# Reload of the residual tile moved into the second batch's turn of the next group

## The reference

```
x = x + L0(x)      # per batch, one of 16 matrices 32x32 mixes the 32 rows
x = x + L1(x)      # x @ base_weight.T + bias + a low-rank adapter per batch
x = x + L2(x)      # paged attention, below
x = x + L3(x)      # as L0, with other weights

# L2: 32 query heads, 8 key/value heads, D = 128, fp32
q, k, v = x @ Wq.T, x @ Wk.T, x @ Wv.T          # q and k: RMS norm, then rotary embedding
kc, vc  = k_cache[block_table], v_cache[block_table]   # 16 pages of 32 positions per batch
scores  = q @ concat(kc, k).T * SCALE           # cached positions >= cache_seqlens are masked
o       = softmax(scores) @ concat(vc, v)
return    o @ Wo.T
```

## Time and profile before

| | us |
|---|---|
| median of 3 runs | 2405.72 |
| lowest and highest | 2402.29, 2407.57 |
| profiled execution | 2406.59 |
| its span | 2404.8 |
| PE busy | 2278.3 (95%) |
| DVE busy | 1766.7 (73%) |
| ACT busy | 1592.9 (66%) |
| mean granted TensorE clock | 0.975 |

### The profile page before, as it was taken

The page is one execution under the profiler, slowest core; times in us unless marked ns, Lnnn a source line. Parts: engine busy times, 40 slices in busy tenths (PEclk is TensorE's granted clock), DMA queues, the critical chain, the costliest instruction groups (busy, mean ns, idle before and its releaser), DMA issues.

```text
span 2404.8 us, 56518 instructions
## 1 busy us (share of the span) xinstructions
PE 2278.3 (95%) x15392; PEld 2026.5 (84%) x15392; DVE 1766.7 (73%) x5613; ACT 1592.9 (66%) x4413; POOL 543.0 (23%) x712
## 2 busy tenths in 40 slices
PE   8999999999998999989989989989989989999999
PEld 5688888888887898988988988988988989887777
DVE  3425777777778987977978978978878878876232
ACT  4324666666668887877877877877877878776221
POOL 1003444444442122111121221212212212110000
PEclk9999999999999999999999999999999999999999
DMA  4335333333348777676777777767767677774332
GB/s 164 94 109 163 101 98 101 119 99 98 101 123 282 251 253 233 225 253 221 233 244 237 225 230 249 232 218 247 234 221 257 216 230 246 224 237 173 112 131 100
DMA packets 347991, 456.02 MB, mean 190 GB/s; under 512 B 34538, under 2 KB 280874, under 8 KB 343726
## 3 DMA queue, kind: packets, MB, share of 16 engines
q1 hardware_dynamic: 308430, 315.83, 41.9%
q0 software_dynamic: 36864, 134.23, 16.4%
q10 hardware_dynamic: 2528, 4.29, 0.5%
HBM read 374.53 MB, written 79.69 MB: 189 GB/s over the span
## 4 chain that ended last, share of the span: by engine, by line
PE 61%; SPq 14%; DMA 9%; issue 8%; DVE 4%; ACT 3%; POOLq 0%; ACTq 0%; POOL 0%; DVEq 0%
PE oP L1209 11%; PE S L1209 10%; PE oP L1285 9%; SPq L379 8%; PE S L1303 7%; PE S L1252 7%; PE bank L1133 5%; DMA x_d<-regC 4%; SPq L377 4%; PE bank L1316 4%; DMA regK<-kT_cache 3%; PE oP L1133 3%; PE oP L1163 2%; DVE k_lo L998 2%; PE oP L1295 1%
## 5 line engine op out<-in xcount | busy, mean ns | idle before, releaser
L1285 PEld LDWEIGHTS oP<-regC,regK 128*128 128x128 f32 x4096 | 540.1, 195 | 37.4 <-issue 4.4
L1285 PE MATMUL oP<-regC,regK 128*128 128x128 f32 x4096 | 552.9, 279 | 1.1
L726 ACT CAST k_hi<-regK 128x544 fp32r<-128x544 f32 x512 | 331.3, 647 | 213.6 <-DMA regK<-kT_cache 109.3
L998 DVE TENSOR_TENSOR k_lo<-regK,k_hi 128x544 fp32r<-128x544 f32 x512 | 368.1, 719 | 98.5 <-ACT k_hi L726 98.3
L1013 DVE CUSTOM_DVE_ANT_0 regC<-S,mask 128x544 f32<-128x544 f32 x512 | 368.5, 720 | 73.1 <-issue 69.5
L1133 PE MATMUL bank<-ident,regC 128*128 128x128 f32 x2048 | 315.2, 277 | 84.9 <-ACT regC L786 84.9
L740 ACT ACTIVATE regC<-regC,nmx 128x544 f32<-128x544 f32 x512 | 387.7, 757 | 4.5 <-DVE nmx L1013 4.0
L1133 PEld LDWEIGHTS bank<-ident,regC 128*128 128x128 f32 x2048 | 247.9, 143 | 87.7 <-issue 87.7
L567 POOL TENSOR_TENSOR regC<-regC 128x256 f32<-128x256 f32 x320 | 245.2, 786 | 278.9 <-DVE regC L973 278.9
L786 ACT COPY regC<-bank 128x512 f32<-128x512 f32 x512 | 298.7, 583 | 5.0 <-PE bank L1133 5.0
L549 POOL DMA_INDIRECT regK<-v_cache,idx x256 | 266.6, 1042 | 91.8 <-issue 91.4
(11 more groups left out here) (136 smaller groups left out, 4319.7 us busy)
## 6 DMA issues: line engine op xcount, KB each, us to landing
regK<-kT_cache SPq DMA_DIRECT2D x1024, 128.0 KB
qkT_d<-regC SPq DMA_DIRECT2D x160, 256.0 KB, 2.3
regC<-qkT_d SPq DMA_DIRECT2D x64, 512.0 KB, 7.1
oT_d<-regC SPq DMA_DIRECT2D x64, 256.0 KB, 6.0
regK<-oT_d SPq DMA_DIRECT2D x16, 1024.0 KB, 5.2
regC<-wqk SPq DMA_DIRECT2D x10, 1024.0 KB, 5.2
v_d<-regC SPq DMA_DIRECT2D x32, 256.0 KB, 2.3
regK<-qkT_d SPq DMA_DIRECT2D x64, 128.0 KB
```

Source lines behind the costliest of these rows:

```text
L726: nc.scalar.copy(k_hi[u % 2].rearrange("p (s t) -> p s t", t=PSIZE), k_sb[b][:, :, h, :]).then_inc(s_khi, 1)
L998: nc.vector.tensor_tensor(lo, k_sb[b][:, :, h, :], hi.bitcast(F32), ALU.subtract).then_inc(s_klo, 1)
L1285: last = nc.tensor.matmul(oP[:, at:at + P], v_sb[b][:, m, h * D:(h + 1) * D], pT_sb[u % 2][:, m * P:(m + 1) * P], start=(h < 4 and m == 0) ...
```

## The change

In turn 3 the reload of x2r is taken out, with its wait on the store. In its place turn 1 of the next group loads x2_d[g - 1], ahead of the store of o_st, with a wait for the count that the store of turn 3 and the table have reached by then. In group 0 turn 1 only waits for its table. The last tile is reloaded after the last group, with a wait for the store as before. The page table of the next group is loaded in turn 0 in place of turn 2, so its count is reached before turn 1 waits.

```
+                    if k == 0 and not last:
+                        load_table(g + 1, 1 - par, BT * NPP)
+                    if k == 1 and first:
+                        sp.wait_ge(s_x2yst, 16)
+                    elif k == 1:
+                        sp.wait_ge(s_x2yst, g * 32 - 16 if last else g * 32)
+                        sp.dma_start(x2r, x2_d[bass.ds(g - 1, 1)].rearrange("a p n -> p (a n)")).then_inc(s_x2r, 16)
                     sp.wait_ge(s_ost, g * BT + (k + 1))
                     sp.dma_start(oT_d[bass.ds(g, 1), :, k, :].rearrange("a p n -> p (a n)"), o_st).then_inc(s_ostst, 16)
...
-                    if k == 2 and not last:
-                        load_table(g + 1, 1 - par, BT * NPP)
                     if k == 3 and not first:
                         sp.wait_ge(s_x2y, g)
                         sp.dma_start(x2_d[bass.ds(g - 1, 1)].rearrange("a p n -> p (a n)"), x2r).then_inc(s_x2yst, 16)
-                    if k == 3:
-                        sp.wait_ge(s_x2yst, g * 32 if last else g * 32 + 16)
-                        sp.dma_start(x2r, x2_d[bass.ds(g, 1)].rearrange("a p n -> p (a n)")).then_inc(s_x2r, 16)
...
             group(NT - 1, 1, False, True)
+            sp.wait_ge(s_x2yst, 32 * NT - 32)
+            sp.dma_start(x2r, x2_d[NT - 1]).then_inc(s_x2r, 16)
```

## The result

| | before | changed |
|---|---|---|
| median, us | 2406.64 (2402.29 to 2407.8, 4 runs) | 2330.79 (2330.29 to 2334.92, 4 runs) |
| ratio, 95% | | 0.9692 [0.9675, 0.9709] |
| span of the profiled execution, us | 2404.8 | 2329.3 |

The change saves 75.8 us, not the 112 that were forecast. 2331 lies outside the range (2286 to 2314) and inside the rival "half relief" (2302 to 2345, priced at 2321). I compare the two profiled executions by their spans: 75.5 us between them.

A forecast was written before the change was run, and what follows sets the result against it. SP's wait for the x2r store was taken to make turn 0's K pages late, stalling ACT and PE at 14 group ends: 2406.6 − 114.4 + 2.0 = 2294.2, forecast 2294 us, range 2286 to 2314.

The forecast's parts named there:

- half relief: Rival: turn 0's pages stay late in the six groups with a loop jump; 2321 us, from 2302 to 2345, chance 0.19.
- the term for what stays at the six jumps: Turn 0 behind SP's loop jumps: PE still waits 0 to 0.7 us, about 0.35 × 6 = 2 us stay.
- The wait removed, and its price: SP's wait for the x2r store before turn 0: 106.5 for 14 stalls' periods plus 7.9, together 114.4 us saved.
- The gap at the jump: SP's loop jump before L388: 3.70 us without a wait, bounds 0.3 and 7.4; L384 then 1.6 us behind its consumer.
- Pages took 19.8 us from L384 to the cast here and 20.8 us at the next group end.: Turn 0's K pages, from load to ACT's cast: the same times were assumed after the change, ready at 1027.1 to 1028.1.
- PE absorbs about 1.5 us: At group ends PE stops less long than ACT waits for K pages; about 1.5 us of ACT's wait is absorbed.
- The store's landing: Landing of the x2r store: trace's 7.2 us average taken over the skill's 2.6 us, which would give back only 36 us.
- The added reload and the moved table: Reload of x2r in turn 1 and page table in turn 0: no cost, given 4 us of slack in each turn.
- the slower rival: Rival: turn 1's reload lands after the residual step needs it, stalling DVE; 2434 us at a 42 us landing, chance 0.02.

The follow-up runs named there:

- e3: Changed kernel with POOL holding the value gathers behind a group's last batch until the next group's query load has landed; 2431.37 us, ratio 0.985, slower kind of chip.
- e8: Changed kernel with SP's loop over groups 1 to 14 written out, on the first kind of chip; 2292.81 us, ratio 0.9529.
- e10: Changed kernel with SP's loop written out and ten tiny transfers ahead of turn 0's own K load, L384 6.0 us late; 2451.34 us, ratio 0.9916.
- e9: Changed kernel with SP's loop written out and five tiny transfers ahead of turn 0's own K load, L384 3.1 us late; 2407.66 us, ratio 0.9725.
- e13: Changed kernel with SP's loop written out and three tiny transfers ahead of turn 0's own K load, L384 1.8 us late; 2399.41 us, ratio 0.9711.
- e7: Changed kernel with POOL holding turn 0's gathers until that batch's K pages have landed, loop jump kept; 2296.16 us, ratio 0.9541.
- e12: Kernel before, store wait and jump kept, with POOL holding turn 0's gathers until the K pages have landed; 2424.62 us, ratio 0.9806.
- e2: Kernel before with SP's loop written out, store wait kept, first run of this edit; 2410.38 us, ratio 0.9773, slower kind of chip.
- e11: Kernel before with SP's loop written out, store wait kept, second run of this edit; 2410.61 us, ratio 0.9755.
- e15: Kernel before with SP's loop written out, store wait kept, third run of this edit; 2408.23 us, ratio 0.9752.
- e18: Kernel before, unaltered, traced on the slower kind of chip; 2465.65 us in one run.
- e17: Changed kernel, unaltered, on the slower kind of chip; 2431.78 us, ratio 0.9864.
- e16: Changed kernel with SP's loop written out and no extra transfers, reference on the slower kind of chip; 2376.93 us, ratio 0.9614.
- e5: Changed kernel, unaltered, run again on the first kind of chip; 2328.41 us, ratio 0.9677.

## Why the prediction was wrong

The wait that the change removes and its price were right. What failed is the term for what stays at the six jumps, put at 2 us and measured at 38.7: SP's gap there was taken at 3.7 us where it is 6.3 to 7.3, and the pages behind it at 19.8 to 20.8 us where they take 21.6 to 22.8.

- **The wait removed, and its price.** Right. Less the 38.7 us that stayed, the 114.4 us are in the measured span to 0.2 us. The stalls at the eight plain ends are gone, L384 there waits for DVE, and the 15th wait kept its 2.1 us.
- **The gap at the jump, "I take the value of the rows, 3.7".** Wrong: 6.3 to 7.3 us. It stood in the prediction that the jump moves out of a quiet stretch into the gathers, with 7.4 us as the upper end. I took the value that I had read, in the quiet stretch. e3 shows that the gathers make the difference (3.4 to 3.6 without them, though on the slower kind of chip). The Trainium skill (Runtime: NRT & Kernel Launch, "Instruction fetch mechanics") has the instructions behind a jump out of the two pages held fetched by DMA. The traces agree: each jump's gap has a packet of 8 KB of instructions, the 135 packets of q14 on the profile's page are 113 with the loop written out (e8), and the price goes with what the DMA engines carry. With it L384 is 3.5 to 4.4 us behind its consumer at the jumps instead of 1.6, 2.3 us more on average.
- **"Pages took 19.8 us from L384 to the cast here and 20.8 us at the next group end."** This step failed as well, and by nearly as much: it needed 21.6 to 22.8 us, 22.1 on average. ACT's lateness of 5.8 us on average is 3.9 of L384 and 22.1 of the pages, less the 20.2 us that ACT leaves; the forecast had 1.6 and 19.8 to 20.8. The two rows were of turns that began 6 to 9 us late, and the third, 19.6 us in group 0, was of a turn in time. I took the value between them for a turn that was late by little, but there it is not between them. Issued into the gathers, the pages take 21, 22 and 23 us at a lateness of 6.0, 3.1 and 1.8 us (e10, e9, e13), and 16.1 to 16.7 with the gathers held (e7, e12). The rival carried the right sentence ("an early start is not passed on in full") and I did not put it into the sum. What it is worth with the gap as forecast is known only roughly. 23 us for the pages would make ACT 4.4 us late and PE 2.9, so my estimate is 6 × 2.9 × 1.35 = 23 us in place of 2, or 2315. In e13, with L384 about as late as I had forecast, the kernel loses 22.5 us in 15 delayed turns, which is 9 us for six, on a kind of chip where ACT wants the pages later. So the term of 2 us was wrong by itself, but whether it alone would have led out of the range is open.
- **The price of half relief, 2321.** Its upper end for the gap was right, but 19.8 us for the pages again made it 10 us too low: per jump ACT is 5.4 to 6.8 us late rather than 4.9, and the batch 5.6 to 7.2 us longer rather than 4.6.
- **"PE absorbs about 1.5 us".** Right: ACT waited 5.39 us, PE 3.87.
- **The store's landing.** The sentence that the slow stores "share the rings with the stores and gathers before them" is wrong as to the gathers: the profile's page has SP's transfers on q1 and the gathers on q0. What they share is the 16 DMA engines. That this makes a store's landing 7.2 us was not tested, and the sum doesn't need it. The formula of the Trainium skill quoted there (DMA: Bandwidth & Descriptors) is fitted to transfers of the software queue, which this store isn't; the one quiet store is all that compares with it here, 2.1 us against 2.6.
- **The added reload and the moved table.** Right. No wait at L455. Its transfer and the residual step behind it, in the reload's line and on DVE's timeline of the changed kernel:

```profile
DMA to landing us min/median/max: 4.1/6.2/7.7
```
```profile
1074.79 0.68 DVE L1040 TENSOR_TENSOR regC<-bank,regC 128x512 f32<-128x512 f32 x1
```

  No idle time stands ahead of L1040, so the slower rival is dead. e8 is near 2294 with the same reload in place, which leaves nothing for it to cost.
- **The chances.** Half relief had 0.19. The argument against it, that consumer-gated turns have the same gathers beside them and hardly stall, missed that those turns issue their pages ahead of the burst (928.4 against a gather at 927.3) and a turn 3 us later issues them into it.

## What to carry to other kernels

A transfer's duration read in a late turn holds for that lateness alone. Before using it for an earlier start, look at what shares the DMA engines with it then; here a later start was passed on to the landing by only a little over half, and the first 2 us were the dearest. A loop jump on the queue that issues loads has a price which depends on the traffic beside it. Where the loads have slack behind it, it costs nothing (e7 has the same gap of some 6 us and batches of 21.25); where they have not, write the loop out or keep the burst away.

## What the runs showed that was not expected

- A jump of SP's loop holds SP for 3.3 to 3.7 us with little beside it and for 5.5 to 7.3 us behind four indirect gathers, and the profile shows the packet of instructions for which it waits; written out, 0.05 us.
- Sixteen pages are ready 16.1 to 16.7 us after L384 with the gathers held, and 18.9 to 23.6 us when issued into them, mostly the more the earlier within the burst.
- Chips differ: the same kernel takes 2406 us on some and 2465 to 2474 on others. Each chip came up in one group of runs only, so the moment isn't ruled out as the cause. On the slower, ACT waits 1.5 to 3 us about once a batch for a signal of PE that comes late. Its cause is open.
- Also open: on the slower kind of chip, writing SP's loop out is worth 57 to 64 us in the kernel before (e2, e11, e15), though L384 comes only 3 us sooner at the jumps and no sooner at the other group ends. ACT's waits for pages fell with it from 52.5 us (e18) to 30.0 (e15), and its waits for the late signal of the scores from 82.8 to 57.7. It is the same in the changed kernel, 53 us between the profiled executions of e17 and e16, where ACT waited 5.2 us for pages. By the ruler, 40 of the 60 us between e18 and e15 and 31 of the 54 between e17 and e16 lie in batches that do not stand behind a group end. So something other than the pages of turn 0 gains by it there. On the first kind the changed kernel shows nothing of this (e5, e8), and the kernel before was not run there with its loop written out.
